# Causal masks of two score passes carried by 30 spare contraction rows, with identity products over 38 instead of 128 columns

## The reference

```python
k = proj(W_key); q = proj(W_query); v = proj(W_value)      # each times 256 ** -0.5
scores = jnp.einsum('bhqd,bhkd->bhqk', q, k) * hd ** (-0.5)
causal = jnp.tril(jnp.ones((t, t), dtype=bool))
scores = jnp.where(causal, scores, -jnp.inf)
weight = jax.nn.softmax(scores, axis=-1)
out = jnp.einsum('bhqk,bhkd->bhqd', weight, v)
```

## Time and profile before

| | |
|---|---|
| median of 3 runs | 1057.14 us (1056.68 to 1058.02) |
| the profiled execution | 1056.73 us |
| its span | 1054.9 us |
| mean granted clock of TensorE | 0.99 |
| PE busy in the span | 1005.0 us (95%) |
| DVE, ACT, POOL busy | 504.5, 508.1, 192.3 us |
| first pass: products, mask products | 512 and 352 |
| second pass: products, mask products | 512 and 320 |

### The profile page before, as it was taken

How to read it: one execution, slowest core, us unless ns; L and a number is a source line. 1 busy time by engine, 2 the same in 40 slices (tenths; PEclk the granted TensorE clock), 3 DMA queues, 4 the chain that set the end, 5 groups by cost and what they waited for, 6 DMA issues and landing times.

```text
span 1054.9 us, 20171 instructions
## 1 busy us (share of the span) xinstructions
PE 1005.0 (95%) x6554; PEld 687.8 (65%) x6554; DVE 504.5 (48%) x1167; ACT 508.1 (48%) x1378; POOL 192.3 (18%) x225
## 2 busy tenths in 40 slices
PE   6999999999999997999999999999999999999985
PEld 3677777777778773665764765765665665666653
DVE  5032113312124455565665665665665566566541
ACT  3344444444444332465465465465465465454433
POOL 5020111101001023213213213213204204200000
PEclk9999999999999998999999999999999999999999
DMA  8422111103100155341451451451352263234110
GB/s 255 151 70 70 59 50 57 54 31 117 52 30 31 54 164 103 101 121 32 145 145 30 132 158 30 112 167 40 93 179 48 71 190 58 71 99 92 32 41 21
DMA packets 68024, 93.79 MB, mean 89 GB/s; under 512 B 11920, under 2 KB 54416, under 8 KB 67984
## 3 DMA queue, kind: packets, MB, share of 16 engines
q1 hardware_dynamic: 61568, 88.44, 29.9%
q10 hardware_dynamic: 6416, 4.85, 1.5%
HBM read 59.41 MB, written 33.59 MB: 88 GB/s over the span
## 4 chain that ended last, share of the span: by engine, by line
PE 84%; DVE 5%; ACT 3%; issue 2%; ACTq 1%; DMA 1%; POOL 0%; DVEq 0%; POOLq 0%
PE PS L887 26%; PE PS L1168 7%; PE PS L1065 6%; PE PS L1117 6%; PE PS L1098 5%; PE PS L1133 5%; PE PS L874 4%; PE PS L1031 3%; PE PS L1199 3%; PE PS L1052 3%; DVE nm L1969 3%; PE PS L1010 2%; PE PS L1119 2%; PE PS L1155 2%; PE PS L1177 1%
## 5 line engine op out<-in xcount | busy, mean ns | idle before, releaser
L887 PE MATMUL PS<-arena 128*128 128x256 f32 x1024 | 314.0, 421 | 0.0
L1969 DVE TENSOR_REDUCE nm<-PS 128x1 f32<-128x512 f32 (+3 forms) x352 | 207.2, 635 | 93.1 <-PE PS L1119 93.0
L1519 ACT ACTIVATE arena<-PS 128x512 f32<-128x512 f32 x256 | 152.1, 600 | 168.7 <-PE PS L1155 168.4
L1365 ACT ACTIVATE arena<-PS 64x8 f32<-64x8 f32 x512 | 88.1, 172 | 193.3 <-PE PS L874 189.9
L874 PEld LDWEIGHTS PS<-arena 128*72 128x72 f32 x1024 | 129.0, 141 | 69.9 <-ACT arena L1365 6.8
L887 PEld LDWEIGHTS PS<-arena 128*128 128x128 f32 x1024 | 155.5, 192 | 0.0
L1133 PE MATMUL PS<-Q,K 98*128 98x512 bf16 (+3 forms) x512 | 120.5, 301 | 8.3 <-ACT arena L1519 4.6
L874 PE MATMUL PS<-arena 128*72 128x8 f32 x1024 | 122.2, 191 | 0.0
L1117 PE MATMUL PS<-K,Q 96*128 96x256 bf16 (+3 forms) x512 | 114.1, 306 | 6.4 <-DMA K<-qk_d 4.6
L1739 DVE SCALAR_TENSOR_TENSOR arena<-arena 128x512 f32<-128x512 f32 x16 | 11.1, 694 | 224.3 <-ACT arena L1376 224.3
L1119 PE MATMUL PS<-negmask,identb 128*128 128x128 bf16 (+2 forms) x352 | 87.4, 248 | 0.0
(11 more groups left out here) (233 smaller groups left out, 1293.8 us busy)
## 6 DMA issues: line engine op xcount, KB each, us to landing
qk_d<-QB SPq DMA_DIRECT2D x21, 512.0 KB, 3.1
Q<-qk_d SPq DMA_DIRECT2D x32, 192.0 KB, 3.8
K<-qk_d SPq DMA_DIRECT2D x31, 192.0 KB, 4.2
gt_d<-arena SPq DMA_DIRECT2D x16, 256.0 KB, 2.5
wx_d<-arena SPq DMA_DIRECT2D x16, 256.0 KB, 2.4
XT<-xt_d SPq DMA_DIRECT2D x8, 512.0 KB, 4.2
GT<-gt_d SPq DMA_DIRECT2D x8, 512.0 KB, 5.8
WX<-wx_d SPq DMA_DIRECT2D x8, 512.0 KB, 6.6
```

What stands on the lines that cost most here:

```text
L887: mm = pe.matmul(o, lhs, rhs, start=first, stop=last, skip_group_check=True)
L1365: s_.activation(HB[0:ST, nxt], PS[0:ST, 7, 0:B], ACT.Tanh).then_inc(c_h.sem, 1)
L1519: s_.activation(PR[:, g % 2, j, at:at + T], PS[:, bank, :], ACT.Exp, scale=SCORE_SCALE).then_inc(t_e.sem, 1)
L1969: v_.tensor_reduce(nm[:, g, h:h + n, i], PS[:, u % 3, 0:n * (i + 1) * P].rearrange("p (n w) -> p n w", n=n), AX.X, ALU.max, negate=True).t ...
```

## The change

Each 128x128 diagonal block needs its mask. The change writes constants into the 30 contraction rows that `KM = 98` leaves free. Row 98 + r of `Q6` has, in every block of 128 queries, 2^60, 2^8, 2^-44 at queries 3r, 3r+1, 3r+2 and 0 elsewhere. The same row of `K6` has -2^66 at all keys past 3r+2, and -2^-38, -2^14 at keys 3r+1, 3r+2. The product is at most -2^22 where a key is later than its query and no more than 2^-30 in size where it is not, for the first 90 queries of a block. The last 38 keep the identity product, now 38 columns wide.

Only a diagonal block may contract over these rows. So a product that held a diagonal block and others is split: the diagonal block over 128 rows, the others over 96 (first pass) or 98 (second pass). Of each 16 products of a stage and pass, 12 become two. Rows 96 and 97 now count in the first pass too and must be 0 there, so POOL clears them (`clear_maxima`) when the second pass of the batch before has ended, and PE waits for `q_z` ahead of a group's first tile. `SCORE_SCALE` moves from the exponential into the query weights. At the start POOL makes the constants, and DVE copies them into `K6` and `Q6` in place of one memset.

```diff
+RUN = 3
+EDGE = RUN * (P - KM)
+Q_STEP = [2.0 ** (60 - 52 * i) for i in range(RUN)]
+K_STEP = [2.0 ** (52 * i - 90) for i in range(RUN)]
+K_PAST = 2.0 ** 66
...
         @block.gpsimd
+            g_.memset(q_steps[:, :], 0.0).then_inc(const, 1)
+            g_.memset(k_steps[:, :], 0.0).then_inc(const, 1)
...
+            for i in range(RUN):
+                if i:
+                    pool.wait_ge(steps, 2 * i)
+                g_.affine_select(out=q_steps[:, :], in_=q_steps[:, :], compare_op=ALU.not_equal, fill=Q_STEP[i],
+                                 base=RUN * KM - i, pattern=[[1, P]], channel_multiplier=-RUN).then_inc(steps, 1)
...
+            def clear_maxima(b, g, earlier):
+
+                pool.wait_ge(t_mm.sem, t_mm.at(b, (g + 1) * TQ))
+                pool.sem_inc(q_free, 1)
+                pool.wait_ge(*earlier)
+                pool.sem_inc(q_free, 1)
+                g_.memset(Q6[KS:KM, g * GH:(g + 1) * GH, :], 0.0).then_inc(q_z.sem, 1)
+                pool.wait_ge(q_z.sem, q_z.at(b, g + 1))
+                pool.sem_inc(q_free, 1)
...
         @block.tensor
                 if u == 0:
                     pe.wait_ge(q_ld[g].sem, q_ld[g].at(b, 2 * len(BLOCKS)))
+                    pe.wait_ge(q_z.sem, q_z.at(b, g + 1 - G))
...
-                w = (i + 1) * P
+                w = i * P
                 for e in range(n):
-                    mm = pe.matmul(PS[:, bank, e * w:(e + 1) * w], Q6[0:KS, g * GH + h + e, i * P:(i + 1) * P],
-                                   K6[0:KS, g * GH + h + e, 0:w], start=(e == 0), stop=False)
-                mm = pe.matmul(PS[:, bank, 0:n * w].rearrange("p (n w) -> p n w", n=n)[:, :, w - P:],
-                               identb[:, :], negmask[:, :].unsqueeze(1).to_broadcast([P, n, P]),
+                    hd, at = g * GH + h + e, e * (w + P)
+                    if i:
+                        pe.matmul(PS[:, bank, at:at + w], Q6[0:KS, hd, w:w + P], K6[0:KS, hd, 0:w],
+                                  start=(e == 0), stop=False)
+                    pe.matmul(PS[:, bank, at + w:at + w + P], Q6[:, hd, w:w + P], K6[:, hd, w:w + P],
+                              start=(i == e == 0), stop=False)
+                mm = pe.matmul(PS[:, bank, 0:n * (w + P)].rearrange("p (n w) -> p n w", n=n)[:, :, w + EDGE:],
+                               identb[:, :], negmask[:, EDGE:].unsqueeze(1).to_broadcast([P, n, P - EDGE]),
                                start=False, stop=True)
...
-                w = T - kt * P
-                pe.matmul(PS[:, bank, at:at + w], K6[0:KM, h, kt * P:(kt + 1) * P],
-                          Q6[0:KM, h, kt * P:T], start=first, stop=False)
+                k, q, w = kt * P, (kt + 1) * P, T - (kt + 1) * P
+                pe.matmul(PS[:, bank, at:at + P], K6[:, h, k:q], Q6[:, h, k:q], start=first, stop=False)
+                if w:
+                    pe.matmul(PS[:, bank, at + P:at + P + w], K6[0:KM, h, k:q], Q6[0:KM, h, q:T],
+                              start=False, stop=False)
...
-                pe.matmul(edge, identb[:, :], negmask_t[:, :].unsqueeze(1).to_broadcast([P, n, P]),
+                pe.matmul(edge[:, :, EDGE:], identb[:, :],
+                          negmask_t[:, EDGE:].unsqueeze(1).to_broadcast([P, n, P - EDGE]),
                           start=False, stop=True).then_inc(t_mm.sem, 1)
...
         @block.vector
-            v_.memset(K6[KS:P, :, :], 1.0).then_inc(init, 1)
+            dve.wait_ge(steps, 2 * RUN)
+            v_.memset(k_steps[KS:KM, :], 1.0).then_inc(init, 1)
+            dve.wait_ge(init, 7)
+            v_.tensor_copy(K6[KS:P, :, :].rearrange("p h (i k) -> p (h i) k", k=P),
+                           k_steps[KS:P, :].unsqueeze(1).to_broadcast([P - KS, H * NT, P])).then_inc(init, 1)
```

More of the change, by code:

```diff
@@ L212, in two_layers @@
         const = sem("const")
+        steps = sem("steps")
         init = sem("init")
@@ L291, in two_layers @@
         q_mm = count("q_mm", 4)
+        q_z = count("q_z", G, credit=G)
+        q_free = sem("q_free")
         q_e = count("q_e", 4)
@@ L601, in _ @@
             g_ = nc.gpsimd
-            for s in (b_rs, b_mr, b_sc, n_mr, y_p, s_p, p_xn, p_hq, p_sg, n_rs, d_p, *c_u, *c_hs):
+            for s in (b_rs, b_mr, b_sc, n_mr, q_z, y_p, s_p, p_xn, p_hq, p_sg, n_rs, d_p, *c_u, *c_hs):
                 pool.sem_inc(s.sem, s.credit)
@@ L624, in _ @@
                              pattern=[[1, P]], channel_multiplier=-1).then_inc(const, 1)
-            pool.wait_ge(const, 13)
+            pool.wait_ge(const, 15)
             g_.tensor_copy(identb[:, :], ident[:, :]).then_inc(const, 1)
+            for i in range(RUN):
[3 more added lines that the diff above has]
+                                 base=RUN * KM - i, pattern=[[1, P]], channel_multiplier=-RUN).then_inc(steps, 1)
+                if i == 0:
+                    g_.affine_select(out=k_steps[:, :], in_=k_steps[:, :], compare_op=ALU.is_ge, fill=-K_PAST,
+                                     base=RUN - 1 - RUN * KM, pattern=[[-1, P]], channel_multiplier=RUN
+                                     ).then_inc(steps, 1)
+                else:
+                    g_.affine_select(out=k_steps[:, :], in_=k_steps[:, :], compare_op=ALU.not_equal, fill=-K_STEP[i],
+                                     base=RUN * KM - i, pattern=[[1, P]], channel_multiplier=-RUN
+                                     ).then_inc(steps, 1)
             for i in range(B):
@@ L759, in roots, with stage2 @@
                                  ).then_inc(d_p.sem, 1)
+            def clear_maxima(b, g, earlier):
[6 more added lines that the diff above has]
+                pool.sem_inc(q_free, 1)
             def stage1(b, more, more2):
+                if more:
+                    clear_maxima(b, 0, (n_mr.sem, n_mr.at(b + 1, 2)))
                 if more2:
                     add_final(b + 2)
-            def stage2(b, more):
+            def stage2(b, more, more2):
                 if more:
+                    clear_maxima(b, 1, (p_hq.sem, p_hq.at(b + 2, 1)) if more2 else (q_z.sem, q_z.at(b, 1)))
                     roots(b + 1)
             def stage3(b, more2):
+                clear_maxima(b, 2, (d_p.sem, d_p.at(b + 1, 1)))
                 if more2:
@@ L773, in stage3, with stage0 @@
                     add_bias(b + 2)
-            def stage0(b, more):
+            def stage0(b, more, first=False):
+                if not first:
+                    clear_maxima(b - 1, 3, (p_xn.sem, p_xn.at(b + 1, 1)) if more else (q_z.sem, q_z.at(b - 1, 3)))
                 if more:
@@ L789, in _ @@
             add_bias(1)
-            stage0(0, True)
+            stage0(0, True, first=True)
             with pool.Fori(0, B - 2) as b:
                 stage1(b, True, True)
-                stage2(b, True)
+                stage2(b, True, True)
                 stage3(b, True)
@@ L1515, in exp @@
                                   PS[:, bank, :].rearrange("p (a b) -> p a b", a=2),
-                                  ACT.Exp, scale=SCORE_SCALE).then_inc(t_e.sem, 1)
+                                  ACT.Exp).then_inc(t_e.sem, 1)
                 else:
```

21 lines of the change are left out of this document (14 added, 7 removed).

## The result

The changed kernel takes 1048.52 us (median of 5 runs, 1047.1 to 1050.37); beside it the kernel before took 1056.68 (5 runs). The ratio is 0.9926, 95% interval 0.9914 to 0.9938: 0.7% faster. The direction was right, but the gain is 8.2 us where 19.3 were forecast.

A forecast was written before the change was run, and what follows sets the result against it. PE, busy 95% of the span, was taken as the bound. It saves 4.28 us a round and keeps 2.52; seven rounds keep 17.6, with the rest 19.3 us, so 1038 us against 1057.1, range 1029 to 1050.

The forecast's parts named there:

- The 38-column slot: On PE, a bf16 mask product of 38 columns takes 0.025 us from its start to the next.
- the fixed cost: On PE, each added product of a split costs about 3 ns beyond its columns.
- u = 4 of stage 2: Sign: this PE tile starts on a wait for DVE, with nothing in hand; 0.22 us saved ahead is lost.
- the transposition of the maxima in stage 0: Sign: this PE step, behind DVE's unbroken reductions, waits 0.4 to 0.5 us longer; 0.46 us of savings is lost.
- the wait at the end of stage 3: Sign: PE's wait of 0.70 us there, amid steps waiting for DVE or ACT, grows by about 0.3 us.
- The list of what DVE and ACT take back: Over stages 0 to 3, 1.76 of PE's 4.28 us saved a round is lost in waits, 2.52 kept.
- step 1: In PE's product costs, weight loads are hidden, so a product costs its columns at 2.4 GHz plus 2 to 4 ns.
- the forecast's stage sums: Time kept per stage in a middle round: 0.61, 0.67, 0.85 and 0.39 us in stages 0 to 3.
- step 2: In stage 2, only 0.22 us is lost, saved by k = 0, one tile and u = 3 before u = 4.
- step 3: A chance of 0.09 that TensorE's clock falls where PE's waits grow, giving 1050 us.
- The second rival: TensorE's clock falls at stage 3's end, 1.7 us each, once in each of seven rounds: 12 us, 1050; chance 0.09.
- the likeliest case: The forecast itself, 1038 us with its own span of 1034 to 1043; chance 0.52.

The follow-up runs named there:

- e4: The changed kernel with masks of all 128 columns again, split products and clears kept: 1060.01 us, ratio 1.0025 to the kernel before.
- e6: The changed kernel with the mask in the middle of each tile and SyncE's group 1 loads issued later: 1041.5 us, ratio 0.9857 to the kernel before.
- e5: The changed kernel with SyncE's six group 1 loads held until group 3's maxima transfer has landed: 1045.59 us, ratio 0.9897 to the kernel before.
- e9: The changed kernel with unread 512-column products in two PE waits, one before stage 1's distances, six in the last batch's stage 1: 1045.07 us.

## Where the prediction was right and wrong

**Right.** The 38-column slot (0.025 us), the fixed cost (3 ns taken, 2 measured), the splits without gaps. The waits came where it put them: u = 4 of stage 2 now waits 0.17 us for DVE, the transposition of the maxima in stage 0 waits 0.19 (0.4 to 0.5 was said); the wait at the end of stage 3 stayed at 0.7 (0.3 more was said). The clears on POOL take the 1.8 us that I had taken, PE has no wait for `q_z`, and e4 shows no cost in the middle rounds. First POOL's group, then the two waits in the timeline:

```profile
L792 POOL MEMSET Q<- 2x2048 bf16 x28 | 50.4, 1799 | 107.4 <-PE PS L1205 107.4
```

```profile
745.92 0.28 PE L1175 MATMUL PS<-ident,nm 128*16 128x128 f32 x1 [0.19 <-DVE nm L2027]
...
777.08 0.10 PEld L1163 LDWEIGHTS PS<-K,Q 96*128 96x128 bf16 x1 [0.17 <-DVE nm L2027]
```

The list of what DVE and ACT take back (1.76 us a round) fits as a sum: e6 keeps 2.7 a round where it left 2.5. Its items were not tested one by one, and two of the waits grew less than said, as above.

**Wrong, step 1: "the loads are hidden".** The step looked at the loads of the identity and of `nm`, at 99 and 90 ns, and asked only what the short mask itself costs. The work behind most tiles is f32, and its loads take 190 ns. The mask that went had been their cover. In the trace the f32 groups are 0.9 us a round longer. Price on the path, as the forecast's stage sums less what e5 keeps: 0.24 us in stage 0, then 0.07, 0.30 and 0.11, 0.7 a round, 5 us in all. With the mask in the middle (e6 against e5) 0.9 a round comes back, this and what the kernel before had exposed.

**Wrong, step 2: stage 2 has only u = 4 to lose.** PE's k = 0 tile had almost nothing in hand against the maxima's transfer: in the middle rounds of the kernel before it started 0.14 to 0.35 us behind the landing, where 0.12 is what it takes after a wait. In the first round, where it started 0.12 behind, the stage took 18.28 us instead of 17.98. I never listed the waits for DMA. Price: 0.3 to 0.5 us a round, 3 us in all.

**Wrong, step 3: the clock at 9 in 100.** The second rival was right in kind. It put the falls at the end of stage 3 and at 1.7 us in each round. They came at the end of stage 1, in two rounds, and in the last batch; the median mean clock went from 0.992 to 0.986, and e9 gives 3.4 us back.

5, 3 and 3.4 are 11.4 us, and 11.1 are missing (19.3 less 8.2). The match to 0.3 is luck: the first price is itself read off the forecast's sums, the clock's part differs from run to run, and some of its 3.4 us may have been lost before the change too. The time lay inside the range (1029 to 1050) only through the rivals that widened it, and outside the likeliest case's own (1034 to 1043).

## What to carry to other kernels

A product that you shorten may have been the cover of the weight load behind it: read the load of what follows, and put the longest product of a group last, ahead of the slowest load. When one engine gets faster, list every wait with nothing in hand, DMA landings too, and ask which traffic the earlier moment meets. Where PE waits, a few products that nothing reads can pay, if the clock at the place is seen to fall.

## What the runs showed that I had not expected

- A 4 KB transfer landed 1.7 to 1.8 us behind its issue with SyncE's queue empty. At the end of stage 2 it took 1.7 to 2.2 us before the change, with three or four loads (64 to 192 KB) still in flight. After it, it took 2.2 to 3.0 with four or five, and 1.8 in the two rounds whose clock had fallen, with one or two. It landed behind the last of them each time; issuing it 0.5 us earlier made the stage only 0.15 us shorter.
- A group of f32 products with 128x128 weights and 256 or 512 columns takes 0.08 us longer behind a 38- or 76-column bf16 product, and 0.05 behind 128 columns, than behind 256 or more, where PE does not wait for another engine. That bf16 loads are faster agrees with the Trainium skill (TensorE: Matmul & The Clock Gate, section Weight-path perf modes — Fast Weight Load (FWL) and DoubleRow), which has the fast load for types other than FP32: 99 against 190 ns here.
- With the same program order, masks of 38 columns instead of 128 (e4 against the changed kernel) lowered the median mean clock from 0.992 to 0.986. PE's waits for the transfer are not the reason: e5 lists none and has 0.987. The reason was not found.
